# Differential attention with a mixture of experts: scaling shared between GpSimd and VectorE, split weights stored and reloaded, feed-forward preparation moved

## What is computed

```python
xn = layernorm(X)
Q, K = xn @ Wq + bq, xn @ Wk + bk                # 16 heads, 128 wide: two halves of 64
A1, A2 = Q1 @ K1.T / 8, Q2 @ K2.T / 8            # 1024 x 1024 each, for each head and batch
P = softmax(A1) - lam * softmax(A2)
Y = concat(P @ V) @ Wo + bo
attn = layernorm(Y, gamma, beta) * 0.2
h = gelu(xn @ W1 + b1); ffn = a * main(h) + (1 - a) * sum(gate * expert(h))
out = X + attn + ffn
```

## Time and profile before

| | us |
|---|---|
| three runs | 1198.51, 1203.36, 1203.72 |
| their median | 1203.36 |
| the profiled execution | 1199.68 |
| its span, first to last instruction | 1197.9 |
| TensorE busy in the span | 1133.8 |
| GpSimd busy | 1017.1 |
| ScalarE busy | 953.5 |
| VectorE busy | 905.3 |

### The profile page before, as it was taken

How to read it: one execution, slowest core, us unless ns; L and a number is a source line. 1 busy time by engine, 2 the same in 40 slices (tenths; PEclk the granted TensorE clock), 3 DMA queues, 4 the chain that set the end, 5 groups by cost and what they waited for, 6 DMA issues and landing times.

```text
span 1197.9 us, 28095 instructions
## 1 busy us (share of the span) xinstructions
PE 1133.8 (95%) x9730; PEld 762.1 (64%) x9730; DVE 905.3 (76%) x1573; ACT 953.5 (80%) x1711; POOL 1017.1 (85%) x657
## 2 busy tenths in 40 slices
PE   5899999999999999999999999999999999997998
PEld 3666666665666666666666666666666666664797
DVE  8877887777787888878788888888888878873510
ACT  3288888888888889898888888888989888884432
POOL 3599999999999999999999999999999999999000
PEclk9989999999999999999999999999999999998999
DMA  8832122221022212222221112221122222100000
GB/s 203 321 80 51 45 50 49 49 49 33 22 49 49 49 44 49 50 49 49 49 49 36 28 40 49 49 49 45 48 49 50 49 49 50 36 10 1 1 19 18
DMA packets 74134, 63.41 MB, mean 53 GB/s; under 512 B 45172, under 2 KB 63092, under 8 KB 74100
## 3 DMA queue, kind: packets, MB, share of 16 engines
q1 hardware_dynamic: 73092, 62.78, 20.9%
q10 hardware_dynamic: 880, 0.19, 0.1%
q0 software_dynamic: 128, 0.01, 0.0%
HBM read 19.96 MB, written 9.44 MB: 25 GB/s over the span
## 4 chain that ended last, share of the span: by engine, by line
PE 55%; POOL 19%; ACT 12%; DVE 7%; issue 6%; ACTq 0%; DMA 0%; DVEq 0%; SPq 0%; POOLq 0%
PE ps L518 18%; PE ps L550 16%; POOL p_mix L431 10%; PE ps L536 9%; ACT work L736 7%; POOL work L428 5%; PE ps L472 3%; ACT p_mix L736 3%; DVE small L930 3%; PE ps L635 3%; PE ps L562 2%; PE ps L622 2%; ACT pt L749 1%; DVE pt L886 1%; POOL w L406 1%
## 5 line engine op out<-in xcount | busy, mean ns | idle before, releaser
L930 DVE TENSOR_REDUCE small<-ps 128x1 f32<-128x1024 f32 x512 | 614.7, 1220 | 191.4 <-PE ps L518 191.4
L431 POOL TENSOR_TENSOR p_mix<-p_mix,work 128x1024 f32<-128x1024 f32 x256 | 609.1, 2379 | 21.4
L749 ACT ACTIVATE pt<-ps 128x512 f32<-128x512 f32 x512 | 306.0, 598 | 150.4 <-PE ps L536 146.6
L536 PE MATMUL ps<-ident,p_mix 64*128 64x64 f32 x4096 | 353.0, 227 | 15.7 <-POOL p_mix L431 13.4
L536 PEld LDWEIGHTS ps<-ident,p_mix 64*128 64x128 f32 x4096 | 304.4, 139 | 69.7 <-issue 53.3
L428 POOL TENSOR_SCALAR work<-work,small 128x1024 f32<-128x1024 f32 x256 | 307.4, 1201 | 33.2 <-DVE small L955 32.4
L736 ACT ACTIVATE p_mix<-ps,small 128x1024 f32<-128x1024 f32 x256 | 286.5, 1119 | 17.3 <-DVE small L930 17.3
L736 ACT ACTIVATE work<-ps,small 128x1024 f32<-128x1024 f32 x256 | 284.7, 1112 | 0.1
L550 PE MATMUL ps<-pt,v_h 128*64 128x512 f32 x1024 | 249.5, 608 | 0.7 <-ACT pt L749 0.7
L518 PE MATMUL ps<-k_hi,q_hi 64*128 64x512 f32 x512 | 228.1, 445 | 10.9 <-ACT p_mix L736 3.7
L518 PE MATMUL ps<-k_hi,q_lo 64*128 64x512 f32 x512 | 226.0, 441 | 0.0
(11 more groups left out here) (135 smaller groups left out, 1242.9 us busy)
## 6 DMA issues: line engine op xcount, KB each, us to landing
qx_hi<-q_hi SPq DMA_DIRECT2D x64, 256.0 KB, 3.7
qx_lo<-q_lo SPq DMA_DIRECT2D x64, 256.0 KB, 4.7
v_scratch<-pt SPq DMA_DIRECT2D x16, 512.0 KB, 4.2
v_h<-v_scratch SPq DMA_DIRECT2D x32, 256.0 KB, 3.1
wqk_raw<-in_L_attn_Wk SPq DMA_DIRECT2D x31, 64.0 KB, 1.8
wqk_raw<-in_L_attn_Wq SPq DMA_DIRECT2D x31, 64.0 KB, 1.9
wo_dup<-in_L_attn_Wo SPq DMA_DIRECT2D x2, 512.0 KB, 8.0
w_raw<-in_L_ffn_W1e SPq DMA_DIRECT2D x4, 256.0 KB, 3.2
```

What stands on the lines that cost most here:

```text
L431: pool.tensor_tensor(e1, e1, e2, ALU.add).then_inc(mix_done, 1)
L536: mm = pe.transpose(pt_ps[:, c * D:(c + 1) * D], p_mix[rows, col:col + P], ident[rows, rows])
L749: act.activation(pt4[:, kb % 2, :, j * P + half * D:j * P + (half + 1) * D], pt_ps.rearrange("p (c q) -> p c q", c=KC), ACT.Copy).then_inc ...
L930: dve.tensor_reduce(neg_max[:, m:m + 1], slot[SLOT[k, s]], AX.X, ALU.max, negate=True)\
```

## The change

There are three parts.

VectorE scales the first 256 of the 1024 columns of each second exponential, in place, right after the sums; GpSimd scales the other 768. The two factors are multiplied beforehand on VectorE (`l1_neg` is now the reciprocal times the first sum times -lam), so both engines apply one factor. VectorE's instruction also writes its row sum to `part_sum`, which nobody reads. GpSimd's addition waits for both shares.

The weights of a head are split once, in the first batch. SyncE stores both parts in a scratch tensor and reloads them for the second batch. Raw, high and low weights have two buffers each (`NW`), and the semaphores for loading and readiness are one per buffer. SyncE's loop is written out.

The feed-forward preparation moves from the tiles 20 to 61 to the tiles 148 to 189, in the second batch. The splitting of W1 in the last head stays.

```diff
--- before.py
+++ after.py
+DVE_KEYS = 256
-COEF_AT, BIAS_AT, SUM_AT, ADD_AT = 20, (21, 22, 25, 26), (28, 29), (33, 36, 41, 44)
-W2_AT = (49, 50, 52, 53, 57, 58, 60, 61)
+COEF_AT, BIAS_AT, SUM_AT, ADD_AT = 148, (149, 150, 153, 154), (156, 157), (161, 164, 169, 172)
+W2_AT = (177, 178, 180, 181, 185, 186, 188, 189)
+NW = 2
+    w_scratch = nc.dram_tensor("w_scratch", (2 * H, P, W_COLS), F32, kind="Internal").ap()
...
-        wqk_raw = sb("wqk_raw", W_COLS)
-        wqk_hi = sb("wqk_hi", W_COLS, F32R)
-        wqk_lo = sb("wqk_lo", W_COLS, F32R)
+        wqk_raw = sb("wqk_raw", 2 * W_COLS)
+        wqk_hi = sb("wqk_hi", NW * W_COLS, F32R)
+        wqk_lo = sb("wqk_lo", NW * W_COLS, F32R)
+        part_sum = small[:, 244:245]
...
-        w_loaded, w_split, proj_mm = sem("w_loaded"), sem("w_split"), sem("proj_mm")
+        w_loaded, w_ready = [[sem(f"{what}{i}") for i in range(NW)] for what in ("w_loaded", "w_ready")]
+        w_split, w_stored, proj_mm = sem("w_split"), sem("w_stored"), sem("proj_mm")
-        scaled, mix_done = sem("scaled"), sem("mix_done")
+        scaled, part_scaled, mix_done = sem("scaled"), sem("part_scaled"), sem("mix_done")
...
+        def raw_w(n, c0, c1):
+            return wqk_raw[:, n % 2 * W_COLS + c0:n % 2 * W_COLS + c1]
+        def w_of(part, n):
+            return part[:, n % NW * W_COLS:(n % NW + 1) * W_COLS]
...
-            def load_w(h):
+            def load_w(n):
+                after(sp, w_ready[n % NW], 32 * (n // NW))
                 for col, src, cols in ((0, Wk, P), (P, Wk, D), (P + D, Wq, P)):
-                    sp.dma_start(wqk_raw[:, col:col + cols],
-                                 src[bass.ds(h, 1), :, 0:cols].rearrange("o e c -> (o e) c")).then_inc(w_loaded, 16)
+                    sp.dma_start(raw_w(n, col, col + cols), src[n, :, 0:cols]).then_inc(w_loaded[n % NW], 16)
+            def store_w(n):
+                sp.wait_ge(w_ready[n % NW], 32 * (n // NW + 1))
+                for i, part in enumerate((wqk_hi, wqk_lo)):
+                    sp.dma_start(w_scratch[2 * n + i, :, :], w_of(part, n).bitcast(F32)).then_inc(w_stored, 16)
+            def reload_w(n):
+                for i, part in enumerate((wqk_hi, wqk_lo)):
+                    sp.dma_start(w_of(part, n).bitcast(F32), w_scratch[2 * (n - H) + i, :, :]).then_inc(w_ready[n % NW], 16)
...
-            sp.wait_ge(w_split, 3)
             load_w(1)
             for i in range(NT):
                 sp.wait_ge(v_evac, 2 * i + 2)
                 sp.dma_start(v_scratch[i, :, :], v_st[:, i % TB, :]).then_inc(v_stored[i % TB], 16)
-            sp.wait_ge(w_split, 6)
-            load_w(2)
+                if i % 2 and i // 2 < NW:
+                    store_w(i // 2)
+                    load_w(i // 2 + 2)
...
+            def prepare(n):
+                par = n % 2
                 sp.wait_ge(lo_done, 2 * n + 1)
                 cross_q(par)
                 after(sp, pv_done, 2 * n - 2)
-                load_v(b, h, par)
-                if isinstance(n, int) and n + 2 >= IT:
-                    return
-                sp.wait_ge(w_split, 3 * n + 6)
-                load_w(next_h)
-            prepare(0, 1, 1)
-            for b in range(B):
-                with sp.Fori(b * H // 2 + (b == 0), (b + 1) * H // 2 - 1) as g:
-                    for par in range(2):
-                        prepare(b, 2 * g + par, par)
-                for par in range(2):
-                    prepare(b, (b + 1) * H - 2 + par, par)
+                load_v(n // H, n % H, par)
+                if NW <= n + NW - 1 < H:
+                    store_w(n + NW - 1)
+                if n + NW + 1 < H:
+                    load_w(n + NW + 1)
+                if H <= n + 2 < IT:
+                    sp.wait_ge(w_stored, 32 * H)
+                    sp.wait_ge(proj_mm, 2 * n + 2)
+                    reload_w(n + 2)
+            for n in range(1, IT):
+                prepare(n)
...
             def split_w(n):
-                pool.wait_ge(w_loaded, 48 * (n + 1))
-                pool.tensor_tensor(wqk_raw[:, 3 * D:], wqk_raw[:, 3 * D:], eighth.to_broadcast([P, P]), ALU.mult)\
+                hi, lo = w_of(wqk_hi, n), w_of(wqk_lo, n)
+                pool.wait_ge(w_loaded[n % NW], 48 * (n // NW + 1))
+                pool.tensor_tensor(raw_w(n, 3 * D, W_COLS), raw_w(n, 3 * D, W_COLS), eighth.to_broadcast([P, P]), ALU.mult)\
                     .then_inc(w_split, 1)
-                after(pool, proj_mm, 2 * n)
-                pool.wait_ge(w_split, 3 * n + 1)
-                pool.tensor_tensor(wqk_hi[:, :], wqk_raw[:, :], zero.to_broadcast([P, W_COLS]), ALU.subtract)\
+                after(pool, proj_mm, 2 * (n - NW) + 2)
+                pool.wait_ge(w_split, 2 * n + 1)
+                pool.tensor_tensor(hi, raw_w(n, 0, W_COLS), zero.to_broadcast([P, W_COLS]), ALU.subtract)\
                     .then_inc(w_split, 1)
-                pool.wait_ge(w_split, 3 * n + 2)
-                pool.tensor_tensor(wqk_lo[:, :], wqk_raw[:, :], wqk_hi[:, :].bitcast(F32), ALU.subtract)\
-                    .then_inc(w_split, 1)
+                pool.wait_ge(w_split, 2 * n + 2)
+                pool.tensor_tensor(lo, raw_w(n, 0, W_COLS), hi.bitcast(F32), ALU.subtract).then_inc(w_ready[n % NW], 32)
...
                     pool.wait_ge(recip_done, 2 * n)
-                    pool.tensor_scalar(e2, e2, l_inv[:, 2 * km + 1:2 * km + 2], l1_neg[:, km % 4:km % 4 + 1],
-                                       ALU.mult, ALU.mult).then_inc(scaled, 1)
+                    pool.tensor_scalar(e2[:, DVE_KEYS:], e2[:, DVE_KEYS:], l1_neg[:, km % 4:km % 4 + 1], None, ALU.mult)\
+                        .then_inc(scaled, 1)
                     pool.wait_ge(scaled, n)
+                    pool.wait_ge(part_scaled, n)
                     pool.tensor_tensor(e1, e1, e2, ALU.add).then_inc(mix_done, 1)
-                if k % TB == SPLIT_W_AT and now(g, k, -2 * TB):
-                    split_w(g * 2 + k // TB + 2)
+                if k % TB == SPLIT_W_AT and g * 2 + k // TB + NW < H:
+                    split_w(g * 2 + k // TB + NW)
                 set_expert(n)
...
-            def proj(n, w, into):
-                pe.wait_ge(w_split, 3 * n + 3)
+                pe.wait_ge(w_ready[par], w_count)
-                        col = half * D if w else 3 * D
+                        col = par * W_COLS + (half * D if w else 3 * D)
...
-                    proj(g * 2 + k // TB + 1, PROJ_AT.index(k % TB), slot[SLOT[k, "proj"]])
...
                     dve.wait_ge(exp_done, 2 * m + 2)
                     after(dve, scaled, m - 3)
                     dve.reciprocal(l_inv[:, r:r + 2], l_sum[:, l:l + 2]).then_inc(recip_done, 1)
-                    dve.tensor_scalar(l1_neg[:, e:e + 1], l_sum[:, l:l + 1], lam_neg, None, ALU.mult)\
-                        .then_inc(recip_done, 1)
+                    dve.wait_ge(recip_done, 2 * m + 1)
+                    dve.tensor_scalar(l1_neg[:, e:e + 1], l_inv[:, r + 1:r + 2], l_sum[:, l:l + 1], lam_neg,
+                                      ALU.mult, ALU.mult).then_inc(recip_done, 1)
+                    part = e2_buf[:, e * S:e * S + DVE_KEYS]
+                    dve.wait_ge(recip_done, 2 * m + 2)
+                    dve.tensor_scalar(part, part, l1_neg[:, e:e + 1], 0.0, ALU.mult, ALU.add, accum_out=part_sum)\
+                        .then_inc(part_scaled, 1)
```

More of the change, by code:

```diff
@@ L286, in _ @@
             load_v(0, 0, 0)
-            def prepare(b, n, par):
-                h, next_h = n - b * H, (n + 2) % H if isinstance(n, int) else n + 2 - b * H
+            def prepare(n):
+                par = n % 2
                 sp.wait_ge(lo_done, 2 * n + 1)
@@ L409, in _ @@
             pool.wait_ge(id_ready, 4)
-            pool.wait_ge(w_loaded, 48)
-            pool.tensor_tensor(wqk_raw[:, 3 * D:], wqk_raw[:, 3 * D:], eighth.to_broadcast([P, P]), ALU.mult)\
+            pool.wait_ge(w_loaded[0], 48)
+            pool.tensor_tensor(raw_w(0, 3 * D, W_COLS), raw_w(0, 3 * D, W_COLS), eighth.to_broadcast([P, P]), ALU.mult)\
                 .then_inc(w_split, 1)
             pool.wait_ge(w_split, 2)
-            pool.tensor_tensor(wqk_lo[:, :], wqk_raw[:, :], wqk_hi[:, :].bitcast(F32), ALU.subtract)\
-                .then_inc(w_split, 1)
+            pool.tensor_tensor(w_of(wqk_lo, 0), raw_w(0, 0, W_COLS), w_of(wqk_hi, 0).bitcast(F32), ALU.subtract)\
+                .then_inc(w_ready[0], 32)
             pool.wait_ge(wv_split, 1)
@@ L418, in _ @@
             start_y()
-            split_w(1)
+            for n in range(1, NW):
+                split_w(n)
             set_main()
@@ L460, in turn_x, with proj @@
                         mm.then_inc(xt_ps, 1)
-            def proj(n, w, into):
+            def proj(n, par, w_count, w, into):
                 t0 = n // H * S
-                pe.wait_ge(w_split, 3 * n + 3)
+                pe.wait_ge(w_ready[par], w_count)
```

(10 more changed lines are left out.)

## The result

The changed kernel takes 1393.74 us in the median of four runs (1391.8 to 1394.72); the kernel before took 1202.21 us beside it (1198.51 to 1203.72). The ratio is 1.160, with a 95% interval of 1.157 to 1.162. The forecast was 1405 us, with a range of 1350 to 1440. The profiled execution took 1391.8 us with a span of 1390.0, so it stands against 1199.68 and 1197.9 before: 192.1 us more between the first and the last instruction.

What follows compares the result with a forecast made beforehand. GpSimd bounds the early heads, TensorE with ScalarE the later; the change makes it all a GpSimd chain. Terms +252.2 + 15.4 - 35.2 - 27.3 = +205.1 us on 1199.7 give 1405 us, range 1350 to 1440.

Steps and rivals of the forecast that it cites:

- What bounds the kernel: GpSimd paces early heads (34.89 us), TensorE with ScalarE later ones (32.29 us); late GpSimd has 0.14 us a tile free.
- The scaling: GpSimd's scaling, 768 columns with one operation: 2.19 us instead of 1.20, +252.2 us over 256 tiles.
- The second wait: GpSimd's addition also waits for VectorE's share: 0.06 us a tile, +15.4 us.
- The splits: Weight splits in the loop fall from 30 to 14, each 2.20 us of GpSimd: -35.2 us.
- The idle time: GpSimd's waits for VectorE's sums in the loop close up once its tile takes 4.67 us: -27.3 us.
- The move: Feed-forward preparation, about 16 us of GpSimd work, moved to tiles 148 to 189: costs and saves nothing.
- VectorE: Its added work per tile, 0.45 to 0.7 us, stays hidden: busy 4.0 of 4.67 us.
- The signs I named: Heads 39.6 and 37.4 us, GpSimd about 96% busy, TensorE under 90%, chain some 85% GpSimd's, addition 0.14 us behind scaling.
- Rivals. 1: GpSimd's cut scaling is fast (0.97 us) and VectorE's share hidden: 1187 us, chance 0.06.
- rival 2: Fast scaling, but VectorE's share delays row maxima on the path: 0 to 32 us above 1187, middle 1203; chance 0.06.
- Rival 3: VectorE's share fights GpSimd for SBUF, held 1.1 us in the mean: 1490 us, chance 0.04.
- Rival 4: TensorE's clock falls while it waits for GpSimd; 7 us spells in every other head: 1453 us, chance 0.05.

Runs made afterwards that it cites:

- split_both: Kernel before with only VectorE's share and GpSimd's one-operation scaling of 768 columns; weights split in both batches, preparation early: 1423.94 us, ratio 1.186.
- prep_early: Changed kernel with the feed-forward preparation back at tiles 20 to 61: 1392.43 us.
- two_ops: Changed kernel with a second multiplication, by 1.0, added to GpSimd's scaling of 768 columns: 1228.42 us, ratio 1.024.
- no_acc: two_ops with VectorE's share writing no accumulator (its addition of 0.0 also removed): 1328.3 us, ratio 1.105.
- no_share: Changed kernel without VectorE's share, GpSimd scaling all 1024 columns by two factors as before: 1191.4 us, ratio 0.993.

## Why the prediction was right, point by point

**What bounds the kernel** held. That GpSimd had 0.14 us a tile to spare, and that anything above it makes the kernel a GpSimd chain, is what happened: all heads, from the first to the last, run at its pace.

**The scaling**, the term that carries the sum, was priced at 2.19 us and measured 2.205. Its count was off: the chain leaves GpSimd after the addition of tile 253, not after the last of 256, which I called 1100.04 us wrongly. So 254 x 1.004 = 255.0 us, where 252.2 stood; the two errors nearly cancel. The prediction also drew on the page "GPSIMD Engine Reference" of the Trainium skill, section "Engine selection", by which one-input operations run at roughly line rate; its estimate from that page was 0.96 us. The two-operation form is near it (0.911 us measured), the one-operation form takes 2.3 times as long (2.205). A forecast by that rule alone would have been 1187 us, with the wrong sign.

**The second wait** was mis-sized: 0.06 us a tile was taken from the weight split, and the runs show none (0.08 us between scaling and addition before and after). 15.4 us too much; the lower bound, 0, was right. The 0.14 us of the split has another cause, which was not tried. The number of waits is not it: in the changed kernel the step that makes the low part waits for one semaphore and follows its forerunner after 0.14 us too (86.34 + 0.72 to 87.20).

**The splits** cost 33.0 us between tile 0 and tile 248 (split_both against the changed kernel) where 35.2 stood. **The idle time** closed by 26.9 of 27.3 us. **The move** cost nothing (prep_early). **VectorE** was hidden, at 0.9 us a tile for sums and share against 0.18: 0.72 more, just above the upper bound of 0.7. It was busy for 393 of the 480 us between 640 and 1120.

Together: 255.0 - 33.0 - 26.9 + 0.3 (a later first scaling) + 0.9 (behind the chain) = 196.3, against 192.1 measured. Most of the remaining 4 us can be read from the timelines: a scaling starts 0.02 us before the recorded end of the addition ahead of it, where it was 0.01 before, 2.3 us in sum, and the additions are 1.0 us shorter in sum (2375 ns in the mean against 2379).

**The signs I named**: heads of 39.36 and 37.18 us (39.6 and 37.4 forecast). The addition starts 0.08 us behind its scaling, not 0.14. TensorE is busy for 86%, under the 90 named. GpSimd is busy for 89% of the span, not 96%: between its first scaling and its last addition it is busy for 98% (1221 of 1248 us), and I forgot the 53 us before and the 90 behind. The chain is GpSimd's for 74%, and for most of the 13% "issue", which I had counted with it.

**Rivals.** 1 and 2 asked what happens if the scaling is fast. two_ops gives the answer: not 1187 to 1219 us but 1228, so the price of VectorE's share in rival 2 was too low (up to 1.0 us a head; measured 33.66 - 32.4 = 1.26). Rival 3's mechanism is real (no_acc), and the form with the accumulator keeps it out. Rival 4's mechanism was seen without its cost. Table by stage of the changed kernel, 400 to 500 and 700 to 800 us, then three pieces behind the end of a head:

```profile
400.00:500.00 100.00, 85.25 (x714) 55.48 (x710) 78.41 (x152) 72.93 (x132) 97.17 (x50) 0.93 0.21 52
700.00:800.00 100.00, 88.29 (x759) 55.11 (x761) 84.14 (x166) 77.58 (x139) 98.25 (x47) 1.00 0.14 36
...
444.00:448.00 4.00, 0.65 (x8) 0.68 (x9) 0.73 (x1) 0.48 (x2) 3.92 (x3) 0.89 0.25 70
448.00:452.00 4.00, 4.00 (x27) 2.96 (x26) 3.26 (x11) 2.96 (x6) 3.92 (x3) 0.68 0.00 0
452.00:456.00 4.00, 4.00 (x39) 2.26 (x38) 3.96 (x6) 3.18 (x6) 3.92 (x2) 1.00 0.00 0
```

In the first batch the granted clock was 0.93, a mix of 2.4 and 1.2 GHz, in the second, without splits, 1.00; over the whole of 400 to 1000 us it was 0.97, so my sign, under 0.95 in that stretch, was not met. The pieces show where it falls: TensorE stood idle for 3.65 us up to 447.35, waiting for GpSimd's addition of a tile behind a weight split, and between 448 and 452 us the granted clock was 0.68, behind that 1.00 again. In split_both, which has splits in the second batch too, it was 0.92 between 700 and 800 us. So the idle time at the splits goes with the lower clock. It cost nothing that the chain shows: GpSimd waited for 0.4 us in the whole loop. TensorE was busy for 85 of 100 us at the lower grant, and waited 13.7 us for GpSimd. The 7 us that the prediction took for a spell stand in no row; the one shown is over before 452 us.

## What to carry to other kernels

Price an instruction by rows of its own form (operation count, kinds of operands), not by its data; on GpSimd a multiplication left out made the same loop dearer. Before moving work between engines, write down how much each has free per tile: here GpSimd had 0.14 us and VectorE 0.7 us a tile, and both moves overran what was there. A part that does nothing alone (the stored weights) can pay together with another (the moved preparation: together 0.7% in no_share), so try them with the bad part taken out before dropping the whole.

## What the runs showed of the hardware

- GpSimd's scaling of 128 partitions, fp32, in place: with one operation 0.914 us for 256 columns, 1.550 for 512, 2.205 for 768, 2.845 for 1024 (2.5 ns a column); with two operations, one factor from memory and 1.0, 0.69 for 512, 0.911 for 768, 1.072 for 960, 1.130 for 1024 (0.86 ns a column); with both factors from memory 1.201 for 1024. Why the form with less to do is slower was not found.
- VectorE's scaling with an accumulator: 279 ns for 64 columns, 479 for 256, and 83 ns for the read. Without it, as a single multiplication, 352 ns for 256, but up to 2504 beside GpSimd; 120 of 256 took over 0.5 us, each to 0.14 to 0.16 us after the end of a GpSimd operation.
- A product of [128 x 1] values with two factors from memory takes VectorE 273 ns, with one 195.
